# Context attention: where VectorE joins a sequence's mix, relative to the maxima of the next sequence

## What is computed

```
x = x + L1_xattn(layernorm(x), ctx_2048, w_qkv, w_proj, b_proj)

q, k, v of the own 32 tokens  = rows of w_qkv, 16 heads of 8 channels
keys and values               = 257 rows of the sequence's context (first 128 channels
                                 the keys, last 128 the values), then the own 32: 289
scores = q k^T / sqrt(8)       per head, 32 x 289
attn   = softmax(scores) v
out    = attn w_proj^T + b_proj
```

## Time and profile before

| | us |
|---|---|
| median of three runs | 3659.68 |
| profiled execution, its own time | 3661.03 |
| its span, first to last instruction | 3659.1 |
| context attention, first scores | 1077.31 |
| context attention, last sequence's scores | 1533.83 |
| context attention, last addition to `x` | 1544.74 |

### The profile page before, as it was taken

One profiled execution on the slowest core, in us unless ns is written; L12 is line 12 of the kernel. 1 busy time (PEld: TensorE's weight loads), 2 busy tenths in 40 slices (PEclk: granted clock), 3 DMA queues, 4 the chain that ended last, 5 costly groups with the idle time before them and its releaser, 6 DMA issues. The chain is left out here.

```text
span 3659.1 us, 108450 instructions
## 1 busy us (share of the span) xinstructions
PE 3278.6 (90%) x40814; PEld 2737.0 (75%) x40816; DVE 2575.0 (70%) x7254; ACT 1817.8 (50%) x4530; POOL 1245.0 (34%) x1823
## 2 busy tenths in 40 slices
PE   6887899999989999897999999999999999874866
PEld 4776889898867777645789898899889899643345
DVE  6784999999968888757565655555655656468765
ACT  3331777777757777664433333333333333224463
POOL 3562888888843333312400000000000000155032
PEclk8997999999989999998799999999999999867687
DMA  4001000000012222200275555555555555254000
GB/s 117 5 0 38 1 0 0 0 0 0 0 48 78 79 78 77 72 1 7 60 139 132 131 132 132 122 139 127 133 131 127 132 130 131 69 108 74 0 3 26
DMA packets 375492, 254.10 MB, mean 69 GB/s; under 512 B 118676, under 2 KB 371560, under 8 KB 374536
## 3 DMA queue, kind: packets, MB, share of 16 engines
q1 hardware_dynamic: 370824, 245.44, 28.0%
q10 hardware_dynamic: 4352, 4.20, 0.5%
HBM read 233.53 MB, written 15.75 MB: 68 GB/s over the span
## 5 line engine op out<-in xcount | busy, mean ns | idle before, releaser
L1062 PE MATMUL psum<-L_ffn_share,L_ffn_prob 128*128 128x128 f32 x4096 | 491.1, 279 | 45.9 <-DVE L_ffn_prob L995 38.3
L1062 PEld LDWEIGHTS psum<-L_ffn_share,L_ffn_prob 128*128 128x128 f32 x4096 | 473.5, 193 | 59.5 <-DVE L_ffn_prob L995 46.2
L878 POOL TENSOR_TENSOR L_ffn_sums<-L_ffn_sims 128x1024 f32<-128x1024 f32 x256 | 485.3, 1912 | 85.8 <-DVE L_ffn_prob L995 85.8
L2463 PE MATMUL psum<-L_xattn_ctxT,L_xattn_q_ctx 128*128 128x257 f32 x2048 | 510.6, 390 | 0.0
L2494 PEld LDWEIGHTS psum<-L_xattn_probT,L_xattn_ctx 32*128 32x128 f32 x16384 | 469.1, 187 | 44.6 <-issue 42.0
L2494 PE MATMUL psum<-L_xattn_probT,L_xattn_ctx 32*128 32x128 f32 x16384 | 493.4, 273 | 2.1 <-DVE L_xattn_probT L2377 2.1
L2315 ACT ACTIVATE L_xattn_prob<-psum,L_xattn_nmax 128x258 f32<-128x258 f32 x512 | 239.2, 472 | 480.1 <-DVE L_xattn_nmax L2363 463.5
L2286 POOL TENSOR_TENSOR L_xattn_z_var<-L_xattn_z_mv,L_xattn_z_eps 128x1 f32<-128x1 f32 x32 | 6.1, 192 | 1248.6 <-DVE L_xattn_z_mv L2389 1219.3
L2463 PEld LDWEIGHTS psum<-L_xattn_ctxT,L_xattn_q_ctx 128*128 128x128 f32 x2048 | 368.5, 191 | 62.2 <-issue 5.9
L920 ACT ACTIVATE psum<-L_ffn_sums,L_ffn_bias 128x512 f32<-128x512 f32 x512 | 339.2, 686 | 89.1 <-DVE L_ffn_prob L995 85.1
L995 DVE SCALAR_TENSOR_TENSOR L_ffn_prob<-L_ffn_sums,L_ffn_best,psum 128x512 f32<-128x512 f32 x512 | 358.1, 741 | 6.9 <-ACT psum L920 3.8
(11 more groups left out here) (459 smaller groups left out, 6651.0 us busy)
## 6 DMA issues: line engine op xcount, KB each, us to landing
L_xattn_ctx<-ctx_dram SPq DMA_DIRECT2D x512, 256.0 KB, 3.9
L_xattn_ctxT<-ctx_T_dram SPq DMA_DIRECT2D x128, 257.0 KB, 3.3
L_xattn_k_all<-ctx_T_dram SPq DMA_DIRECT2D x128, 128.5 KB, 2.1
L_xattn_v_all<-ctx_dram SPq DMA_DIRECT2D x128, 128.0 KB, 2.2
L_attn_qkv_scratch<-L_attn_qkv SPq DMA_DIRECT2D x24, 256.0 KB, 2.8
L_attn_rows<-L_attn_qkv_scratch SPq DMA_DIRECT2D x24, 256.0 KB, 5.3
start_raw<-ctx_dram ACTq DMA_DIRECT2D x16, 256.0 KB, 11.9
L_xattn_v_rows<-L_xattn_v SPq DMA_DIRECT2D x8, 256.0 KB, 2.3
```

Source lines behind the costliest of these rows:

```text
L878: nc.gpsimd.tensor_tensor(sums[:, h % RING, :, :], sx, sy, ALU.add).then_inc(summed, 1)
L1062: last = nc.tensor.matmul(pair(2 * s)[:, c * P:(c + 1) * P], prob[:, h % RING, c * P:(c + 1) * P], share[:, h % RING, :], start=(h == 0 an ...
L2463: last = nc.tensor.matmul(scores(s)[:, g, 0:CTX], q_ctx[:, p, c, b, h:h + 4, :].rearrange("p h n -> p (h n)"), ctxT[:, b, c, :], start=(c ...
```

## The change

VectorE's `maxes` is split into `low_maxes` (groups 0 and 1, behind `scored_low`) and `high_maxes` (groups 2 and 3, behind `scored`). Body n of VectorE is now: the lower maxima of n+1, the join of n-2, the upper maxima of n+1, the inverse of n, the copy of n. The join at the end of the body is gone, and a second one stands behind the loop, for the last sequence but one. Nothing changes on the other engines.

```
+        def two_behind(t, b, before):
+
+            return (t, b - 2) if b >= 2 else (t - 1, b + BT - 2) if before else None
...
-            def maxes(t, b):
+            def low_maxes(t, b):
                 dve.wait_ge(scored_low, t * BT + b + 1)
-                for g in range(G):
-                    if g == 2:
-                        dve.wait_ge(scored, t * BT + b + 1 + BT)
+                for g in (0, 1):
+                    nc.vector.tensor_reduce(nmax[:, b % 2, g:g + 1], scores(g), X, ALU.max, negate=True).then_inc(maxed, 1)
+
+            def high_maxes(t, b):
+                dve.wait_ge(scored, t * BT + b + 1 + BT)
+                for g in (2, 3):
                     nc.vector.tensor_reduce(nmax[:, b % 2, g:g + 1], scores(g), X, ALU.max, negate=True).then_inc(maxed, 1)
...
             def tile(t, before, last):
                 for b in range(BT):
                     if ahead(t, b, last, 1):
-                        maxes(*ahead(t, b, last, 1))
+                        low_maxes(*ahead(t, b, last, 1))
+                    if two_behind(t, b, before):
+                        join(*two_behind(t, b, before), before)
+                    if ahead(t, b, last, 1):
+                        high_maxes(*ahead(t, b, last, 1))
                     invert(t, b)
                     dve.wait_ge(turned1, t * BT + b + 1)
                     nc.vector.tensor_copy(probT[:, b % 2, 1, :, :], turned_bank(1)).then_inc(copied1, 1)
-                    if b:
-                        join(t, b - 1, before)
-                    elif before:
-                        join(t - 1, BT - 1, before)
-
-            maxes(0, 0)
+
+            low_maxes(0, 0)
+            high_maxes(0, 0)
             over_tiles(dve, tile)
+            join(TILES - 1, BT - 2, True)
             join(TILES - 1, BT - 1, True)
```

## The result

| | before | changed |
|---|---|---|
| median | 3659.26 us | 3711.24 us |
| profiled execution, its span | 3659.1 us | 3710.5 us |
| first scores of context attention | 1077.31 us | 1076.78 us |
| last sequence's scores | 1533.83 us | 1587.86 us |
| granted TensorE clock, whole span | 0.932 | 0.937 |

The median of before has one more execution in it than the table ahead of the prediction. The changed kernel takes 1.0148 times as long, 95% interval 1.0127 to 1.0169, that is 47 to 62 us more. The forecast was 3713 us, its range 3697 to 3728. From the first to the last scores of the stage lie 511.08 us instead of 456.52: 54.6 us more, against the 54 of the sum.

What follows compares the result with a forecast made beforehand. TensorE was taken as the bound, with hidden waits for ScalarE's exponentials. A new TensorE-VectorE ring of 3.76 us a sequence, plus 0.20 and 0.84, makes a tile 16.08 us against 14.35: 54 us more, 3713 us, range 3697 to 3728.

Steps and rivals of the forecast that it cites:

- the 54 of the sum: Context attention: a tile of 16.08 us against 14.35, plus 1.73, over 31.25 tiles gives 54 us more.
- The ring: TensorE and VectorE, once per sequence: lower scores, two maxima, join, joined, share and mix, next scores; 3.76 us.
- Gaps: Between starts of successive scores on TensorE: 3.76 us, 3.96 where x is added, 4.60 at the projection.
- Joined to the share: Handoff from the join's last instruction on VectorE to TensorE: 0.05 us, read from a stall in the epilogue.
- Share to next scores: On TensorE, from share matmul to the next scores: 1.13 us, seen once as 1.03.
- The projection's 0.84: Once a tile TensorE's projection goes behind the joined wait and adds 0.84 us.
- the bounds: Shorter last term and handoff: 19 us less together; 0.05 us more at each of two engine crossings: 13 us more.
- an upper pair 0.39 after the lower one: TensorE's upper scores wait for ScalarE 0.39 us instead of 0.87, buried in the new stall before the share.
- VectorE's idle time: It moves from before the join to before the lower maxima, some 0.6 us, released by the scores.
- Rival 1: Early exponentials pay: the join is through before TensorE reaches the share, 12.76 us a tile, 3609 us; chance 2%.
- Rival 2: No change: the path through scores and join is 3.33 us a sequence, 0.43 shorter; 3660 us, chance 3%.
- Rival 3: TensorE's clock falls from standing still more: 3732 us for a tenth of the stage, all 190 more; chance 6%.

Runs made afterwards that it cites:

- in_ring: The changed kernel with one more maximum over 289 constants on VectorE between the lower maxima and the join; 3763.54 us, ratio 1.0268.
- off_ring: The changed kernel with one extra maximum over 289 constants at the end of VectorE's body, behind the copy; 3716.01 us, ratio 1.0149.
- act_after: The changed kernel with one more ScalarE copy of 128x256 constants ahead of the fourth exponential; 3716.32 us, ratio 1.0152.
- early_release: The changed kernel, but the join copies the share out early and TensorE's share and mix wait for that copy; 3689.36 us, ratio 1.0085.
- share_early: The kernel before with TensorE's projection and share matmul moved between lower and upper scores of the next sequence; 3803.64 us, ratio 1.0392.
- after_three: The changed kernel with the join behind three maxima instead of two; 3762.27 us, ratio 1.0271.

## Why the prediction was right

**The ring.** The step that carries the forecast, that joined now hangs on lower scores of the same TensorE body, is what the profile after shows and what in_ring, off_ring and the row of joins behind 0 to 3 maxima test. Gaps forecast at 3.76, 3.76, 4.60 and 3.96 came out as 3.81, 3.87, 4.57 and 3.92.

**Its terms.** Lower scores to lower maxima 0.80 (0.83 forecast), two maxima 0.74 (0.74), join to its last instruction 0.81 (0.82). Joined to the share was 0.05 where x is added or the projection goes first (1310.96 plus 0.19 to 1311.20), but 0.13 in the two other bodies (1307.08 plus 0.19 to 1307.40): the epilogue's 0.05 was not the typical one. The stall there stands twice in the trace of before, not once, the second ahead of the last projection. Share to next scores was 1.13, in one body of four 1.20. The projection's 0.84 was taken from the start of its weight load; its matmul starts at 1302.31, only 0.73 ahead of the share. Behind a stall, though, load and matmul start together, and 0.84 is what the ring paid (1311.20 to 1312.04). The errors are inside the bounds and partly cancel, 0.23 us a tile too little against some 0.15 too much, which is luck: the tile is 16.17 instead of 16.08. The stage grew by 54.6 us, the rest of the program was 3 us shorter in this profiled execution than in the one of before, so the span grew by 51.4.

**What is late next.** Forecast was an upper pair 0.39 after the lower one, hidden under the stall. In the rows the scores last 1.04, 0.96, 0.77 and 1.11 us instead of 0.77, so the upper pair was 0.0 to 0.34 late; the stall was 0.33 to 0.40 in three bodies and 0.78 in the one with the addition. act_after measured that slack: an extra ScalarE instruction brought 0.01 us a tile instead of 0.60.

**VectorE's idle time** moved from the join to the lower maxima as said, 0.59 to 0.73 us and 1.41 behind the projection, which the forecast of 0.6 left out. The new waiting for the join is 58 us, not 50, because the body with the addition waits twice as long as the others.

**The rivals.** Rival 1 needed more than it was given: I priced it at 3609 us for a join that comes in time, and early_release, with 5.0 us of that wait left, is at 3689. My own sum had the reason in it (upper maxima at 2.53) but it did not enter the rival's price. Rival 2 is refuted by the time. Rival 3 did not occur in the changed kernel; with more standing still it did:

```profile
1088.00:1300.00 212.00, 187.24 (x2356) 137.52 (x2352) 159.79 (x487) 152.03 (x526) 71.02 (x211) 1.00 0.25 70
```

```profile
1088.00:1300.00 212.00, 190.04 (x1991) 128.62 (x1993) 139.00 (x407) 128.16 (x441) 59.81 (x177) 0.93 0.21 58
```

The first row is the changed kernel, granted clock 1.00, the second share_early, 0.93 (columns as in rows 1). In the same stretch after_three and in_ring have 0.99, at 2166 and 2168 matmuls instead of 2356, and share_early has 1991. act_after has 0.99 too, at 2347, so one profiled execution of each gives an order and no more. The sentence of the Trainium skill, TensorE: Matmul & The Clock Gate, section What's actually happening, that activity lifts the throttle, agrees with this order. Of share_early's loss the clock is the smaller part: 23 us, read from its slow tiles, against 114 from the ring.

## What to carry to other kernels

When an instruction moves to a later place on its engine, list what stands ahead of it there and ask which of that waits for the engine that waits for the moved one; if both waits are of the same pass, a ring is closed, and its length is a sum that can be read off the trace before anything is built. A busy-looking engine (TensorE at 88% in the changed kernel, 98% before) and idle time on the other (0.66 us a sequence on VectorE) say little about such a ring: work in it cost in full here, work off it nothing. Put the branch of a loop where its engine waits anyway.

## What the runs showed of the hardware that was not expected

The end of VectorE's loop costs 0.26 us of start-to-start time once per tile. Moving it alone, with the order of all instructions kept, took 0.28 us off each tile. The granted clock of TensorE stayed at 1.00 in the changed kernel with waits of 0.3 to 0.8 us in every sequence of 4 us. In in_ring and after_three, with waits of 0.7 to 1.15 us in every sequence, it fell in two and three single tiles, which took 0.4 to 1.6 us longer for it; in share_early it fell in 17 tiles of 30. In act_after, with fewer waits for the join than the changed kernel (28.6 us instead of 61.0), it fell in two tiles as well, so the waits alone do not tell when it falls.
